# Refining the inverse roots on GpSimd: one third-order step in place of two Newton steps

## The reference, cut to what matters

```python
def _rms_norm(x):
    eps = jnp.finfo(x.dtype).eps
    return x * jax.lax.rsqrt(jnp.mean(x * x, axis=-1, keepdims=True) + eps)
...
q = _rms_norm(q)
k = _rms_norm(k)
cos, sin = _polar_rotary(seqlen, HD, q.dtype)
q = _apply_rotary(q, cos, sin)
k = _apply_rotary(k, cos, sin)
```

## Time and profile before

| what | value |
|---|---|
| timed runs, median of 3 | 271.57 us |
| timed runs, lowest and highest | 270.48 and 273.31 us |
| span of the profiled execution | 268.1 us |
| busy share PE, ACT, DVE, POOL | 91%, 84%, 73%, 32% |
| instructions PE, ACT, DVE, POOL | 3663, 330, 746, 241 |

### The profile page before, as it was taken

The page is one execution under the profiler, slowest core; times in us unless marked ns, Lnnn a source line. Parts: engine busy times, 40 slices in busy tenths (PEclk is TensorE's granted clock), DMA queues, the critical chain, the costliest instruction groups (busy, mean ns, idle before and its releaser), DMA issues.

```text
span 268.1 us, 9782 instructions
## 1 busy us (share of the span) xinstructions
PE 245.2 (91%) x3663; PEld 129.2 (48%) x3664; DVE 195.6 (73%) x746; ACT 223.8 (84%) x330; POOL 85.7 (32%) x241
## 2 busy tenths in 40 slices
PE   8359999899999999999999999997998999998980
PEld 4143555546556455464564655644553222223880
DVE  1779579597796977978879779652253777999992
ACT  3267989989999999999999999988864987878685
POOL 8740432425325244162342532512011000000473
PEclk9957999999999999999999999999999999999998
DMA  5303362453626517336155352551300346651045
GB/s 131 84 1 60 62 120 61 84 107 93 117 50 145 105 33 157 78 79 139 42 112 106 90 98 53 124 109 20 71 2 18 75 110 154 149 124 39 19 131 167
DMA packets 58217, 23.60 MB, mean 88 GB/s; under 512 B 42928, under 2 KB 56016, under 8 KB 58192
## 3 DMA queue, kind: packets, MB, share of 16 engines
q1 hardware_dynamic: 57904, 23.24, 39.4%
q10 hardware_dynamic: 288, 0.02, 0.1%
HBM read 5.04 MB, written 2.10 MB: 27 GB/s over the span
## 4 chain that ended last, share of the span: by engine, by line
PE 73%; DVE 8%; ACT 6%; DMA 5%; issue 5%; POOL 2%; ACTq 0%; DVEq 0%; POOLq 0%
PE O L630 10%; PE O L617 10%; PE S L750 8%; PE M L419 5%; DMA qk<-parts 5%; PE S L513 5%; PE S L503 4%; PE M L663 4%; PE S L535 3%; PE M L649 3%; PE S L546 2%; PE S L791 2%; PE S L555 2%; PE O L637 2%; PE S L760 2%
## 5 line engine op out<-in xcount | busy, mean ns | idle before, releaser
L928 ACT ACTIVATE probs_late<-S 128x1024 f32<-128x1024 f32 x64 | 63.4, 1029 | 1.1 <-PE S L535 0.8
L928 ACT ACTIVATE probs_past<-S 128x1024 f32<-128x1024 f32 x64 | 62.4, 1040 | 1.9 <-PE S L503 1.8
L617 PE MATMUL O<-probs_past,values 128*32 128x512 f32 x256 | 34.9, 618 | 1.4 <-ACT o_sb L934 0.7
L1554 POOL TENSOR_TENSOR minus_half_sum<-sum_eps,minus_half 128x40 f32<-128x40 f32 x16 | 4.5, 283 | 73.5 <-DVE estimate L1180 69.7
L1300 DVE TENSOR_TENSOR summed<-M,x_res 128x256 f32<-128x256 f32 x15 | 6.4, 425 | 28.7 <-PE M L663 28.7
L630 PE MATMUL O<-probs_late,mixed 128*32 128x128 f32 x512 | 26.4, 279 | 0.0
L630 PE MATMUL O<-probs_late,values 128*32 128x128 f32 x512 | 25.7, 273 | 0.0
L1429 DVE SCALAR_TENSOR_TENSOR cY<-coup,ratio,Y 128x256 f32<-128x256 f32 x48 | 21.0, 480 | 5.6 <-ACT coup L1028 4.7
L750 PE MATMUL S<-X,cn_w 128*128 128x512 f32 x48 | 25.0, 627 | 0.0
L513 PE MATMUL S<-qk 32*128 32x128 bf16 x512 | 19.0, 219 | 0.3 <-ACT probs_late L928 0.2
L513 PEld LDWEIGHTS S<-qk 32*128 32x128 bf16 x512 | 8.1, 92 | 20.7 <-issue 18.6
(11 more groups left out here) (189 smaller groups left out, 571.9 us busy)
## 6 DMA issues: line engine op xcount, KB each, us to landing
Y<-X SPq DMA_DIRECT2D x48, 128.0 KB, 2.4
xT_in<-in_xT SPq DMA_DIRECT2D x16, 128.0 KB, 2.6
x_res<-in_x SPq DMA_DIRECT2D x16, 128.0 KB, 2.1
out<-result SPq DMA_DIRECT2D x16, 128.0 KB, 1.9
future_in<-in_future SPq DMA_DIRECT2D x1, 256.0 KB, 3.0
qk<-parts SPq DMA_TRANSPOSE x15, 4.9
w_o<-in_w_o SPq DMA_DIRECT2D x2, 64.0 KB, 2.5
cn_w<-in_cn_w SPq DMA_DIRECT2D x2, 64.0 KB, 2.1
```

Source lines behind the costliest of these rows:

```text
L617: mm = pe.matmul(O[32 * g:32 * g + 32, :], values[p][:, 0, g, s, at:at + 32], probs_past[:, s, g, :], start=m == 0, stop=False)
L928: act.activation(dst, S[TILE_BUFFER[n]][:, :, :], ACT.Exp).then_inc(exp_done[n], 1)
```

## The change: what it does

The first guess y and s, the sum of a head's squares with its epsilon, are as before. Where two Newton steps y(1.5 - 0.5 s y^2) followed, one third-order step follows: 3/8 y ((s y^2 - 5/3)^2 + 20/9). Its six instructions are a square, a product, a sum, a square, a sum and the last product into `rstd`. The factor 3/8 isn't multiplied in there; it goes into the rotation table that the host makes. Every instruction now waits for the one before it. The tile `minus_half_sum` and one of the two `estimate` tiles go, and the constant tile `one_half` is replaced by two of its size, which DVE fills at the start.

```diff
-        estimate = [sb(f"estimate{n}", [128, T * (HEADS + G)]) for n in range(NEWTON)]
+        estimate = sb("estimate", [128, T * (HEADS + G)])
...
-        minus_half_sum = sb("minus_half_sum", [128, T * (HEADS + G)])
...
-        one_half = sb("one_half", [128, T * (HEADS + G)])
+        minus_5_3 = sb("minus_5_3", [128, T * (HEADS + G)])
+        plus_20_9 = sb("plus_20_9", [128, T * (HEADS + G)])
...
-            dve.memset(one_half[:, :], 1.5)
+            dve.memset(minus_5_3[:, :], -5.0 / 3.0)
+            dve.memset(plus_20_9[:, :], 20.0 / 9.0)
...
             def refine(count):
 
-                steps = 4 * NEWTON
-                before = steps * (count - 1)
+                before = 5 * (count - 1)
                 done = n_["root_step_done"]
+                y = estimate[:, :]
+                both = lambda a: a.rearrange("p (h o) -> p h o", o=1).broadcast_to([128, T * (HEADS + G), 2])
                 pool.wait_ge(n_["estimate_ready"], count)
-                pool.tensor_tensor(minus_half_sum[:, :], sum_eps[:, :], minus_half[:, :], ALU.mult).then_inc(done, 1)
-                for n in range(NEWTON):
...
+                pool.tensor_tensor(root_sq[:, :], y, y, ALU.mult).then_inc(done, 1)
+                pool.wait_ge(done, before + 1)
+                pool.tensor_tensor(root_step[:, :], root_sq[:, :], sum_eps[:, :], ALU.mult).then_inc(done, 1)
+                pool.wait_ge(done, before + 2)
+                pool.tensor_tensor(root_sq[:, :], root_step[:, :], minus_5_3[:, :], ALU.add).then_inc(done, 1)
+                pool.wait_ge(done, before + 3)
+                pool.tensor_tensor(root_step[:, :], root_sq[:, :], root_sq[:, :], ALU.mult).then_inc(done, 1)
+                pool.wait_ge(done, before + 4)
+                pool.tensor_tensor(root_sq[:, :], root_step[:, :], plus_20_9[:, :], ALU.add).then_inc(done, 1)
+                pool.wait_ge(done, before + 5)
+                pool.tensor_tensor(rstd[:, :, :, :].rearrange("p t h s -> p (t h) s"), both(y), both(root_sq[:, :]),
+                                   ALU.mult).then_inc(n_["rstd_ready"], 1)
...
-    scaled = table[:, ORDER].reshape(2, T, 128, HALF).transpose(2, 0, 1, 3) * np.float32(HALF ** -0.5 * HD ** 0.5)
+    scaled = table[:, ORDER].reshape(2, T, 128, HALF).transpose(2, 0, 1, 3) * np.float32(HALF ** -0.5 * HD ** 0.5 * 0.375)
```

More of the change, by code:

```diff
@@ L57 @@
 TOK = BATCH * SEQ
-NEWTON = 2
 ROOT_BITS = float(0x5F3759DF)
@@ L1126, in estimate_root @@
                 dve.wait_ge(n_["bits_step_done"], b * 3 + 3)
-                dve.scalar_tensor_tensor(out=estimate[0][:, :], in0=bits_step[:, :], scalar=1.5, in1=bits[:, :],
+                dve.scalar_tensor_tensor(out=estimate[:, :], in0=bits_step[:, :], scalar=1.5, in1=bits[:, :],
                                          op0=ALU.add, op1=ALU.mult).then_inc(n_["estimate_ready"], 1)
```

## The result

| | before | after |
|---|---|---|
| timed runs, median | 271.50 us (6 runs, 270.48 to 273.31) | 267.39 us (6 runs, 267.26 to 268.30) |
| ratio, 95% interval | | 0.9837 [0.9802, 0.9872] |
| span of the profiled execution | 268.1 us | 265.2 us |

Each timed run of the changed kernel has a span too: the profiled execution took 267.33 us at a span of 265.2, so 2.1 us lie around the span.

The account below looks back on a forecast made before the run. PE was taken to set the loop's pace, with POOL's roots counting only at the start. Terms 0.69 + 0.20 - 0.17 = 0.72 us off 271.57 gave 270.85 us, range 269.3 to 272.3.

Parts of the forecast that it names:

- The loop: Loop iterations: PE sets 10.88 us and L663's wait covers `rstd`, so roots 0.90 us earlier gain nothing.
- Term 1: First rope at the start: `rstd` comes earlier until DVE's L1137 is late next; gain 0.69 us, bounds 0.5 to 1.0.
- two side effects: First rope: `mix_values` moves onto L1137, losing up to 0.2 us; ropes win up to about 0.3; taken as equal.
- Term 2: Rope of batch 3: `mix_values` ends before it, so the rope runs undisturbed; gain 0.20 us, bounds 0 and 0.2.
- Term 3: PE's half clock near the start: its return may not follow the earlier work; -0.17 us, bounds 0 and -0.34.
- the edit priced at nothing: Tile declarations: one 128x40 tile less moves later tiles' addresses; no row prices it, taken as nothing.
- What it had called covered: Batch 2: ropes end 0.9 us earlier, but DVE then waits for ACT's copy and PE didn't stand there; nothing.
- No cover at the first rope: Rival at the first rope: POOL's 0.90 to 1.55 us counts in full, giving 270.1 us; chance 6%.
- the roots count in every batch: Rival in the loop and late batches: 13 x 0.90 = 11.7 us gained, giving 259.9 us; chance 3%.
- the clock comes back later, slower: Rival at 15 to 28 us: PE's return to 2.4 GHz slips, giving 273.6 us, mid case 272.0; chance 12%.
- No net gain: Rival: L1137's loss, the clock and an unmoved batch 3 DMA leave 0.16 us, giving 271.4 us; chance 15%.

Follow-up runs that it names:

- e8: The changed kernel with three more idle products in the refinements of batches 2 to 15, none in 0 and 1; 268.09 us (4 runs).
- e1: The changed kernel with unused tiles that put every later tile back at its address of before; 269.98 us (12 runs), ratio 0.9942 to the kernel before.
- e3: The changed kernel with 160 unused bytes behind `parts`, so only the DMA source keeps its new address; 267.35 us (6 runs), ratio 0.9834 to the kernel before.
- e5: The changed kernel with 128 unused bytes behind `parts`, so `parts` and `qk` both start at a multiple of 256 bytes; 267.50 us.
- e2: The kernel before, nine-instruction refine kept, with only `minus_half_sum` declared last, so `parts` starts at a multiple of 256; 269.11 us (7 runs), ratio 0.9906.
- e13: The kernel before with PE's idle time at the start filled with idle matmuls; 271.21 us (12 runs), ratio 0.9994 to the kernel before.
- e14: The changed kernel with `parts` alone at a multiple of 256 (as e3) and PE's idle start filled with idle matmuls; 267.11 us (6 runs).
- e9: The changed kernel with more idle matmuls on PE at the start (18 and 12 in place of 4 and 4); 267.02 us (4 runs).
- e10: The changed kernel with three more idle products in the refinement of batch 2 alone; 267.97 us (6 runs).
- e11: The changed kernel with three more idle products in the refinements of batches 3 to 15 only; 267.93 us (6 runs).

## Why the prediction was wrong, point by point

**The loop** was right: iteration 10.88, the residual sum's wait in front of the rope, `rstd` 0.9 earlier to no use. e8 confirms it.

**Term 1**, 0.69 us, was right to the digit: PE's first transposes follow POOL's first instruction by 5.40 us in place of 6.09 (15.82 - 9.73), and DVE's L1137 is late next. Its two side effects both came and nearly cancel, as assumed. L1137 takes 0.88 where it took 0.71, and the three ropes 0.68 where they took 0.79. The 0.17 lost is less than the whole instruction of `mix_values` that the prediction thought possible (two of them take 0.89). POOL itself started 0.42 earlier in the profiled execution (9.31 against 9.73); e1 has 9.96 and e3 9.67, so that is scatter.

**Term 2**, the rope of batch 3, was right in mechanism and size (0.69 against 0.89, 0.16 us at PE in e1), but in the changed kernel it hardly counts, as the DMA behind it has become shorter.

**Term 3** was right in mechanism: the clock's return doesn't follow the work, and the loss of 0.19 us in e5 and 0.27 in e1 lies inside its bounds of 0 and 0.34. Its half us for each us at half clock is the upper end of the 0.3 to 0.5 that the traces give. In the trace of the result the return happened to go along, from 23.4 to 22.4, and only 0.04 us was lost (1.11 at the transposes, 1.07 at L663) where 0.17 was forecast. The bounds left out that the clock can also come back earlier than the work moves, as in e3, where it gave 0.44.

**The step that failed** is the edit priced at nothing: "One 128x40 tile less moves the addresses of later tiles; no row prices it, and I take nothing." It moved the source of 15 transposing DMAs to a multiple of 256 bytes and brought their median landing from 4.9 to 4.2 us. In the loop that is covered. Before batch 3 and batch 15, where the landing takes 6.6 and 6.4 us and PE already stood idle 0.92 and 0.99, it is not the earlier trace rows. e2 prices it at 2.3 us of 4.1. The rows had shown both waits, so time off these two DMAs was worth as much at PE, up to the length of the waits; what was missing was any price of an address.

**Where the miss lies in the traces.** The forecast was 0.72 us off the span and 2.9 came. The start gave 1.07 where 0.69 - 0.17 = 0.52 was forecast, and 0.42 of these 0.55 us is POOL's earlier start, which is luck. Batch 3 gave 0.99 where 0.20 was forecast, batch 15 gave 0.75 where nothing was.

**What the trace of before didn't show.** The forecast of 270.85 us is the timed median 271.57 less 0.72, and that base was sound: six runs have 271.50. But the timed runs gained 4.1 us and the traces 2.9. The runs beside e1 have 24 spans of the kernel before, with a median of 269.35, and the profiled execution at 268.1 lies below all of them. So the rows come from an execution that was 1.2 us shorter than usual, and what cost the usual ones that much couldn't be read there. Of the 3.5 us between span and median, 2.1 lie around the span, and the rest is this.

**What it had called covered** was batch 2, on the word of one execution in which its DMA landed after 4.9 us. The refinement alone gives 1.4 us in medians (e1), of which the first rope gives 0.7, less what the clock takes back (0.27 in its trace), and batch 3's rope 0.16. How much of the rest comes from batch 2, how much from the clock, stays open.

**The rivals.** "No cover at the first rope" and "the roots count in every batch" are ruled out by the traces and e8. Of "the clock comes back later, slower" the mechanism is real, but at 0.3 to 0.5 us for each us it outweighed the gain in none of the traces. "No net gain" did not come either. None of the four named an address, so the right answer lay outside all of them.

## What to carry to other kernels

A change that adds or drops a tile has a second effect: it moves every tile declared behind it, and a DMA that reads small blocks from one of them can become slower or faster. Compare the DMAs' landing times before and after each edit, and pin such a source to a good boundary, so that the next edit doesn't undo it. When a wait of PE for a DMA stands in the trace at all, the DMA's own length is worth as much as anything ahead of it, and one profiled execution does not say how long it takes in the others. Look whether a packet of the instruction queue falls into it. And an edit that is meant to take one cost away, like the idle matmuls here, must be looked at in its own trace before its time is read as that cost.

## What the runs showed of the hardware

A transposing DMA from SBUF to SBUF of 128 x 2560 bf16 took 4.1 to 4.2 us to land when its source started at a multiple of 256 bytes, and 4.9 when it started 32, 128 or 160 past one; the target's start (0, 32 or 128 past) made no difference. Its packets of 256 bytes, away from the late landings, took 17.9 ns in the mean from a multiple of 256 and 21.3 to 21.8 off one (batch 6).

A few of the 15 DMAs land later than the rest: that of batch 3 in every trace (5.6 to 5.9 us at the good addresses; 6.6 at the bad ones, 5.7 in e13), that of batch 15 in all but e13 and e14 (5.2 to 5.8 at the good addresses, 4.8 in e9; 6.4 to 6.5 at the bad ones; e13 has 4.8 and e14 4.4), those of batches 1 and 2 in some traces and not in others, and that of batch 4 in e9 and e13 (5.9 and 6.7). Every one that landed 0.7 us or more after the median of its trace had a 16 KB packet of the instruction queue under way, but not every one with such a packet landed late. The experiments didn't vary that.

In the stage from 15 to 23 us PE lost some 0.3 us for each us more at half clock (e1, e5) and gained 0.4 to 0.5 for each us less (e3, e10, e11). The half clock came back in e9 and e13 after PE had stood idle for 1.85 and 3.10 us, and did not in e14 after 1.87.

Where GpSimd's `mix_values` ran beside VectorE's ropes or L1137, these took longer: four ropes 0.86 to 0.94 us in e11 against 0.69, two instructions of L1137 0.88 against 0.71.
